# Attention on one Trainium2 core: value products for four heads at once, and softmax sums from one product of added probabilities

## The chip, the cores and the metric

The kernel runs on one core of a Trainium2 chip. The metric is the time on the device in microseconds (us), start to end of the program. The engines are TensorE (PE), VectorE (DVE), ScalarE (ACT), GpSimd (POOL) and SyncE (SP), which here only issues transfers. An instruction stream is one per engine, in order; the engines meet through semaphores.

## What is computed

A two-layer model on 4 batches of 512 tokens, width 512. The part that matters here is the attention of the second layer: 16 query heads in 4 groups, which share 4 key and value heads of 32 columns, with a linear bias by distance and a key mask. Cut from the reference:

```python
# _L1_xattn_ref: Q per query head, K and V per group, one group per key head
...
scores = scores + m * rel[None, None, None]
neg = jnp.finfo(scores.dtype).min
scores = jnp.where(mask[:, None, None, None, :], scores, neg)
w = jax.nn.softmax(scores, axis=-1)
out = jnp.einsum('bghqk,bkgd->bqghd', w, V)
out = out.reshape(b, q_len, G * Hpg * dh)
return out @ Wo
...
x = x + jnp.tanh(g_xattn[1]) * _L1_xattn_ref(_layernorm(x, axis=-1), ctx_2048, ctx_2048, mask_BxS2_bf1, L1_xattn_Wq, L1_xattn_Wk, L1_xattn_Wv, L1_xattn_Wo)
```

Before it come a cross attention stand-in (a product of quantised matrices) and a ternary feed-forward; after it a mixture of experts. The change touches neither.

## The kernel before

**Blocks and steps.** `stage_attention` works through 16 blocks: 4 batches times 4 values of j; a block is the four heads g = 0..3 that have their own key head g and query head j. A block has 8 steps (`BLOCK = 2 * KB`), a batch 32 (`STEPS`). In the kernel before, a step treats one pair of heads (`PAIRS = ((0, 2), (1, 3))`) and one key tile k of 128 keys: steps 0 to 3 are the four key tiles of the first pair, steps 4 to 7 those of the second.

**A step on PE** (L1355 to L1378) makes the two score matmuls of its pair, keys down and queries across, into `p_col` (L1371); between and after them it makes some of the *row scores* of a later block (`row_scores`, L1321), queries down, only to find each query's maximum; then the value products of the step before (`values`, L1334), and at last the fills of this step. There are two buffers each of `p_col` and `p_row`, so PE waits for ACT's exponential of the step before, and for DVE's maximum of two row scores before. How many row scores a step makes is in `ROWS_AT`; those from step 5 on (`AHEAD`) are for the block after the next.

**Value products.** `v1` holds for each key tile and head 32 columns of values and 32 columns of ones, in f32. Each head's product has 64 output partitions, 32 of the output and 32 of the sum of the probabilities, so two heads fill the 128 partitions of `p_out[pr]`, accumulated over four key tiles:

```python
for c, g in enumerate(PAIRS[pr]):
    mm = nc.tensor.matmul(p_out[pr][c * 2 * DH:(c + 1) * 2 * DH, :], v1[b % 2][:, k, g, :], prob[n % 4][:, c, :],
                          start=(k == 0), stop=(k == KB - 1))
```

**ACT** makes an exponential of 128 x 512 for each score matmul (L1240) into one of four `prob` buffers, copies `p_out` out (`take_out`, L1226), and the high f16 halves of fills. **DVE** makes the maxima of the row scores (`maxima`, L1438), the low halves of fills (`low`), the statistics and normalisation of the next batch's x (L1388 to L1400), and the inverse of the sums (`inverse`, L1451). **POOL** multiplies the output by the inverse and splits it into two f16 halves (`normalise`, L1160 to L1169). **SP** takes the sums out to memory, brings them back spread over 128 partitions, takes the inverses out, and spreads them over the head's rows (`sums_out`, `sums_spread`, `inverse_out`, `inverse_rows`); it also places the maxima (`place_top`, L1080) and the halves of queries and keys (`place`, L1073) into the operands of the scores.

**Fills** (`attention_fills`, L929) are work of the next batch (transposes of the context and x, the products for keys k, values v and queries q) and of the batch before (the output product, y), given to steps of the batch by the tables `NEXT` and `RESULT`. "top" is the transposition of a block's maxima, at step 4. y of a batch waits until POOL has normalised its last block.

**End.** The last block's inverse is made by DVE directly from the copied sums (`last_inverse`, two of its four halves in the last steps) and `last_normalise` multiplies the heads one by one (L1464).

## Time and profile before

| | us |
|---|---|
| median of 3 runs (1326.04 to 1329.34) | 1326.54 |
| the profiled execution, its own time | 1324.98 |
| its span, first to last instruction | 1323.3 |
| PE busy in the span | 1088.6 (82%) |
| DVE busy | 751.8 (57%) |
| ACT busy | 664.9 (50%) |
| POOL busy | 460.1 (35%) |
| granted clock of PE, mean | 0.931 |

The profile is of one execution; 1.7 us of its time lie around its span. The attention blocks stand from 369.9 to 728.0 us of the span. A busy time counts each moment in which the engine has an instruction in work; matmuls overlap, so a mean length of one can be larger than what it adds. The granted clock is 1.00 for 2.4 GHz and 0.5 for 1.2 GHz, averaged over the stretch. A wait is put down to the instruction whose signal came last.

### The profile page before, as it was taken

Reading aid. Unit: us, or ns where it says so; the run is one execution under the profiler, and the core shown is the slowest. Engines: PE = TensorE matmul, PEld = TensorE weight load, DVE = VectorE, ACT = ScalarE, POOL = GpSimd, SP = SyncE. Lnnn points to the kernel's source line nnn. Section 1 sums busy time; section 2 is a strip of 40 time slices with the busy share of each in tenths; the row PEclk is TensorE's granted clock in tenths of the full one; section 3 lists DMA queues with packets and bytes.
Section 4 is the critical chain, followed back from the end, with each engine's and each line's share of the span. In section 5 each row is a group of like instructions: output and inputs, shape, how many; then the busy total and the mean of one; then the engine's idle time right before and its main releaser. Section 6 shows DMA issues by size and latency. Waiting matters only on the chain. (4 is left out here: it accounts for less than half of the span.)

```text
span 1323.3 us, 19258 instructions
## 1 busy us (share of the span) xinstructions
PE 1088.6 (82%) x6093; PEld 520.5 (39%) x6111; DVE 751.8 (57%) x1420; ACT 664.9 (50%) x1010; POOL 460.1 (35%) x503
## 2 busy tenths in 40 slices
PE   0567788896699999999999467899997999999910
PEld 0343444453233343243232133444444566566600
DVE  6889867756786674665653466443333435443224
ACT  6888878794156665655667154212212344334400
POOL 1102443323102332322333303435006888882054
PEclk9978899998989999999999778799998999999965
DMA  9126600001102111110110122024003454442256
GB/s 336 45 96 196 257 0 1 1 1 40 37 23 68 37 40 54 40 37 22 41 31 18 45 74 66 1 96 181 1 0 114 150 162 166 150 156 93 71 170 227
DMA packets 66573, 110.62 MB, mean 84 GB/s; under 512 B 16756, under 2 KB 28660, under 8 KB 65992
## 3 DMA queue, kind: packets, MB, share of 16 engines
q1 hardware_dynamic: 56952, 77.63, 18.2%
q0 software_dynamic: 9264, 31.92, 7.6%
q8 instruction: 37, 0.61, 0.2%
q14 instruction: 32, 0.26, 0.1%
q10 hardware_dynamic: 288, 0.20, 0.1%
HBM read 68.44 MB, written 33.28 MB: 77 GB/s over the span
## 5 line engine op out<-in xcount | busy, mean ns | idle before, releaser
L1240 ACT ACTIVATE prob<-p_col,mask_col,any_key 128x512 f32<-128x512 f32 x256 | 185.7, 778 | 110.4 <-PE p_col L1371 108.9
L1438 DVE CUSTOM_DVE_ANT_0 ajunk<-p_row,mask_row 128x512 bf16<-128x512 f32 x256 | 166.8, 685 | 70.8 <-PE p_row L1321 70.8
L1334 PE MATMUL p_out<-prob,v 128*64 128x512 f32 x512 | 139.0, 621 | 0.1
L1321 PE MATMUL p_row<-ks,early_place 99*128 99x512 f16 x256 | 99.3, 389 | 13.4 <-DVE top L1438 11.9
L1160 POOL TENSOR_TENSOR o<-sum_a,rec 32x512 f32<-32x512 f32 x30 | 37.9, 1264 | 195.2 <-DMA rec<-inv_d 193.0
L1371 PE MATMUL p_col<-early_place,ks 101*128 101x512 f16 x256 | 95.5, 386 | 0.7 <-ACT prob L1240 0.3
L2290 DVE SCALAR_TENSOR_TENSOR shid<-s_up,ssilu 128x352 f32<-128x352 f32 x39 | 20.5, 525 | 122.1 <-PE s_up L2236 122.1
L2258 PE MATMUL s_down<-mw,shT 128*128 (+1 forms) x351 | 82.2, 379 | 1.1 <-ACT shT L2198 1.1
L2236 PE MATMUL s_gate<-mw,sxT 128*128 x468 | 78.3, 318 | 4.2 <-ACT sxT L2204 3.3
L2236 PE MATMUL s_up<-mw,sxT 128*128 x468 | 76.7, 314 | 0.0
L1851 PE MATMUL p_gate<-mw 128*128 128x512 f16 (+1 forms) x288 | 71.7, 402 | 1.2 <-ACT mw L1737 1.2
L1867 PE MATMUL p_down<-mw 128*128 128x512 f16 (+1 forms) x288 | 64.9, 384 | 9.4 <-DVE x L1956 9.4
L2292 DVE TENSOR_TENSOR shidr<-shid,shidr 128x352 f16<-128x352 f32 x39 | 59.7, 1532 | 21.5 <-ACT shidr L2188 21.5
L2151 POOL TENSOR_TENSOR mw<-mstg,mw 128x1408 f32 (+5 forms) x28 | 63.2, 2258 | 8.4 <-POOL mstg L2147 8.4
L1851 PE MATMUL p_up<-mw 128*128 128x512 f16 (+1 forms) x288 | 66.1, 379 | 0.0
L2180 ACT ACTIVATE ssilu<-s_gate 128x352 f32<-128x352 f32 x39 | 18.1, 463 | 95.2 <-PE s_gate L2236 95.2
L525 PE MATMUL po<-ctxT,xT 128*128 128x512 f32 x128 | 63.5, 646 | 0.0
L570 PE MATMUL po<-w2T,ctxT 128*128 128x512 bf16 x241 | 57.1, 379 | 7.7 <-DVE ctxT L791 4.9
L553 PE MATMUL pair<-w1T,q1T 128*128 128x512 bf16 x254 | 59.8, 379 | 1.4 <-DVE w2T L731 1.2
L2236 PEld LDWEIGHTS s_gate<-mw,sxT 128*128 128x128 f16 x468 | 43.8, 99 | 42.1 <-issue 21.8
L1758 ACT ACTIVATE silu<-p_gate,ebias 128x512 f32<-128x512 f32 (+1 forms) x24 | 16.3, 683 | 86.2 <-PE p_gate L1851 86.2
L2146 POOL TENSOR_TENSOR mw<-mstg,up 128x1408 f32 (+5 forms) x28 | 56.3, 2011 | 5.9 <-DMA mstg<-in_L_ffn_gate_w 5.4
(305 smaller groups left out, 2151.6 us busy)
## 6 DMA issues: line engine op xcount, KB each, us to landing
x_slots<-nought SPq DMA_DIRECT2D x3, 3328.0 KB, 19.8
...
```

What stands on the lines that cost most here:

```text
L525: mm = nc.tensor.matmul(po[t % 2][:], xT[b % 2][:, k, t * P:(t + 1) * P], ctxT[b % 2][:, k, :], start=(k == 0), stop=(k == KB - 1))
L553: mm = nc.tensor.matmul(ph[n][:, c:c + D], q1T[:, k, :], w1T[:, k, n * HALF + c:n * HALF + c + D], start=(k == 0), stop=(k == KB - 1))
L1240: nc.scalar.activation(prob[s % 4][:, c, :], p_col[c][:], ACT.Exp, bias=mask_col[:, b, k:k + 1], scale=any_key[:, b:b + 1]).then_inc(t_exp, 1)
L1321: nc.tensor.matmul(p_row[g % 2][:], qs[0:ROWS_R, j, g, t * P:(t + 1) * P], ks[b % 2][0:ROWS_R, g, :], start=True, stop=True).then_inc(t_ro ...
L1334: mm = nc.tensor.matmul(p_out[pr][c * 2 * DH:(c + 1) * 2 * DH, :], v1[b % 2][:, k, g, :], prob[n % 4][:, c, :], start=(k == 0), stop=(k == ...
L1371: nc.tensor.matmul(p_col[c][:], ks[b % 2][0:ROWS_C, g, k * P:(k + 1) * P], qs[0:ROWS_C, j, g, :], start=True, stop=True).then_inc(t_col, 1)
L1438: nc.vector.tensor_tensor_reduce(junk[:, g % 2, :], p_row[g % 2][:], mask_row[:, blk // HPG, :], 1.0, -3e38, ALU.add, ALU.max, top[blk % 2 ...
L1851: mm = nc.tensor.matmul(bank[i % 2][0:rows(m), :], unit(SHARED + n, hs, at + k * EI + m * P, rows(m)), xT[:, hm, k, g * S:(g + 1) * S], st ...
L1867: mm = nc.tensor.matmul(p_down[t % 2][:], hT[n][hs][0:rows(m), m, t * P:(t + 1) * P], unit(SHARED + n, hm, D0 + m * D, D, rows(m)), start= ...
L2151: nc.gpsimd.tensor_tensor(half(e, 1, q), s, half(e, 0, q), ALU.subtract).then_inc(m_wl, 1)
L2236: mm = nc.tensor.matmul(bank[n][:], xT[n][:, hs, k, :], w[:, bass.ds(e * (2 * WC) + c, EI)], start=(k == 0 and hs + hm == 0), stop=(k == K ...
L2258: mm = nc.tensor.matmul(p_down[n][:], hT[n][0:rows(m), hs, m, :], w[0:rows(m), bass.ds(e * (2 * WC) + c, D)], start=(m == 0 and hs + hm == ...
```

## The change

**Steps by key tile.** `PAIRS` is now ((0, 1), (2, 3)), and steps 2k and 2k + 1 treat the two pairs on key tile k. The value products of a key tile are made for all four heads together, once in two steps, in four matmuls of 32 output partitions each, without ones columns, into one `p_out`. There are six `prob` buffers.

**Sums.** The probabilities of the four key tiles are added before they meet PE: POOL adds tiles 0 and 1 (`add_first`, two instructions of 128 x 1024), DVE adds tiles 2 and 3 (`add_next`, four of them). PE multiplies the result by ones in four matmuls into `p_den`, at step 3 of the next block (`SUMS_AT`), ACT copies it (`take_sums`), and one transfer takes the sums out. In the last block tile 3 goes to PE without having been added.

**Also moved:** the tables of fills and rows, POOL's normalisation is one instruction instead of four, DVE's inverse is at step 7 instead of 5, some placings of queries go ahead of the inverses on SP, and the end is made from the new buffers. `v` is plain, 128 columns.

```diff
-    NEXT = {0: ("ctx", 0), 1: ("ctx", 1), 2: ("ctx", 2), 3: ("ctx", 3), 6: ("k", 0), 8: ("x", 0), 9: ("x", 1), 10: ("x", 2),
-            9.5: ("v", 0), 10.5: ("x", 3), 11: ("q", 0), 22: ("q", 1), 26: ("q", 2)}
-    RESULT = {13: 0, 15: 1, 17: 2, 19: 3}
-    OWN_Q, TOP_AT = 4, 4
+    NEXT = {0: ("ctx", 0), 1: ("ctx", 1), 2: ("ctx", 2), 3: ("ctx", 3), 7: ("k", 0), 8: ("x", 0), 9: ("x", 1), 9.5: ("x", 2),
+            10: ("x", 3), 12: ("q", 0), 23: ("q", 1), 25: ("q", 2), 29: ("v", 0)}
+    RESULT = {15: 0, 17: 1, 19: 2, 21: 3}
+    OWN_Q, TOP_AT = 5, 4
...
-    ROWS_AT = (2, 2, 2, 2, 0, 3, 3, 2)
+    ROWS_AT = (1, 3, 2, 2, 0, 3, 2, 3)
     AHEAD = 5
+    SUMS_AT = 3
...
+    def pair_of(blk, k, pr):
+        return prob[(BLOCK * blk + 2 * k + pr) % PROBS]
+    def heads(pr):
+        return prob_sum[:, 2 * pr:2 * pr + 2, :]
...
             def sums_out(n):
-                sp.wait_ge(t_outa, n + 1)
-                sp.dma_start(den_d[n % 2, 0:GROUPS:2, :], sum_a[n % 2][DH:P:2 * DH, :]).then_inc(t_den, 16)
                 sp.wait_ge(t_outb, n + 1)
-                sp.dma_start(den_d[n % 2, 1:GROUPS:2, :], sum_b[n % 2][0:P:2 * DH, :]).then_inc(t_den, 16)
+                sp.dma_start(den_d[n % 2], den_row[0:P:DH, :]).then_inc(t_den, 16)
...
+                for f in soon:
+                    place(f)
                 if blk:
                     inverse_out(blk - 1)
                     inverse_rows(blk - 1)
...
             def normalise(n):
                 pool.wait_ge(t_rec, 64 * (n + 1))
+                pool.wait_ge(t_outa, n + 1)
...
-                for g in range(GROUPS):
-                    q = slice(g * DH, (g + 1) * DH)
-                    nc.gpsimd.tensor_tensor(o[q, :], (sum_a, sum_b)[g % 2][n % 2][q, :], rec[q, :], ALU.mult).then_inc(t_scaled, 1)
...
+                nc.gpsimd.tensor_tensor(o[:], taken[n % 2][:], rec[:], ALU.mult).then_inc(t_scaled, 1)
...
+            def add_first(blk):
+                need(pool, t_over, blk)
+                for pr in range(2):
+                    pool.wait_ge(t_exp, 2 * (BLOCK * blk + 2 + pr + 1))
+                    pool.nop(nofuse=True)
+                    nc.gpsimd.tensor_tensor(heads(pr), pair_of(blk, 0, pr)[:], pair_of(blk, 1, pr)[:], ALU.add).then_inc(t_addp, 1)
             for blk in range(BLOCKS + 1):
+                if blk < BLOCKS:
+                    add_first(blk)
                 if blk > 1:
                     normalise(blk - 2)
...
+            def take_sums(n):
+                act.wait_ge(t_over, n + 1)
+                need(act, t_den, 16 * n)
+                nc.scalar.copy(den_row[:], p_den[:]).then_inc(t_outb, 1)
+            def prob_free(i):
+                blk, inb = divmod(i - PROBS, BLOCK)
+                k, pr = divmod(inb, 2)
+                act.wait_ge(t_pv, KB * blk + k + 1)
+                if k < 2:
+                    act.wait_ge(t_addp, 2 * blk + pr + 1)
+                else:
+                    act.wait_ge(t_addd, 2 * ((KB - 2) * blk + k - 2) + pr + 1)
...
                     if inb == 1 and blk:
-                        take_out(blk - 1, 1)
-                    if inb == KB + 1:
-                        take_out(blk, 0)
+                        take_out(blk - 1)
+                    if inb == SUMS_AT + 1 and blk:
+                        take_sums(blk - 1)
...
             def values(n):
...
+                pe.wait_ge(t_exp, 4 * (n + 1))
...
+                for g in range(GROUPS):
+                    q = slice(g * DH, (g + 1) * DH)
+                    mm = nc.tensor.matmul(p_out[q, :], v[b % 2][:, k, q], pair_of(blk, k, g // 2)[:, g % 2, :],
                                           start=(k == 0), stop=(k == KB - 1))
...
+            def sums(blk, of, start, stop):
+                for g in range(GROUPS):
+                    mm = nc.tensor.matmul(p_den[g * DH:(g + 1) * DH, :], ones[:, 0:DH], of(g), start=start, stop=stop)
+                return mm
+            def sums_of(blk):
+                pe.wait_ge(t_addd, 2 * (KB - 2) * (blk + 1))
+                need(pe, t_outb, blk)
+                sums(blk, lambda g: prob_sum[:, g, :], True, True).then_inc(t_over, 1)
...
-                    if s + b:
-                        values(STEPS * b + s - 1)
+                    if pr == 0 and s + b:
+                        values((STEPS * b + s) // 2 - 1)
+                    if inb == SUMS_AT and blk:
+                        sums_of(blk - 1)
...
+            def add_next(blk, k, pr):
+                i = 2 * ((KB - 2) * blk + k - 2) + pr
+                dve.wait_ge(t_exp, 2 * (BLOCK * blk + 2 * k + pr + 1))
+                if k == 2:
+                    dve.wait_ge(t_addp, 2 * blk + pr + 1)
+                else:
+                    dve.wait_ge(t_addd, i - 1)
+                dve.nop(nofuse=True)
+                nc.vector.tensor_tensor(heads(pr), heads(pr), pair_of(blk, k, pr)[:], ALU.add).then_inc(t_addd, 1)
...
-                    if inb == AHEAD and blk:
+                    if inb == BLOCK - 1 and blk:
                         inverse(blk - 1)
+                    if inb == 0 and blk:
+                        add_next(blk - 1, KB - 1, 1)
+                    if inb in (BLOCK - 3, BLOCK - 2):
+                        add_next(blk, KB - 2, inb - BLOCK + 3)
+                    if inb == BLOCK - 1 and blk + 1 < BLOCKS:
+                        add_next(blk, KB - 1, 0)
```

The order of the instructions, at three places. First PE, steps 5 and 6 of the second block. Before:

```order
L1371 MATMUL p_col<-early_place,ks 128x512
L1321 MATMUL p_row<-ks,early_place 128x512
L1371 MATMUL p_col<-early_place,ks 128x512
L1321 MATMUL p_row<-ks,early_place 128x512
L1334 MATMUL p_out<-prob,v_0 64x512 x2
L1321 MATMUL p_row<-ks,early_place 128x512
L1371 MATMUL p_col<-early_place,ks 128x512
L1321 MATMUL p_row<-ks,early_place 128x512
L1371 MATMUL p_col<-early_place,ks 128x512
L1321 MATMUL p_row<-ks,early_place 128x512
L1334 MATMUL p_out<-prob,v_0 64x512 x2
```

And now, the same two steps:

```order
L1430 MATMUL p_col<-early_place,ks 128x512
L1360 MATMUL p_row<-ks,early_place 128x512
L1430 MATMUL p_col<-early_place,ks 128x512
L1360 MATMUL p_row<-ks,early_place 128x512 x2
L1430 MATMUL p_col<-early_place,ks 128x512
L1360 MATMUL p_row<-ks,early_place 128x512
L1430 MATMUL p_col<-early_place,ks 128x512
L1360 MATMUL p_row<-ks,early_place 128x512
L1373 MATMUL p_out<-prob,v 32x512 x4
```

The value slot is gone from the odd step, and the even step's has four matmuls of 32 partitions for two of 64. (Before, one more row score followed the last row of its piece; step 7 makes it now.)

Second PE, steps 3 and 4 of the third block, where the sums of the block before are made (now):

```order
L1430 MATMUL p_col<-early_place,ks 128x512
L1360 MATMUL p_row<-ks,early_place 128x512
L1430 MATMUL p_col<-early_place,ks 128x512
L1360 MATMUL p_row<-ks,early_place 128x512
L1379 MATMUL p_den<-prob_sum,ones 32x512 x4
L1430 MATMUL p_col<-early_place,ks 128x512 x2
L1373 MATMUL p_out<-prob,v 32x512 x4
```

The slot of the sums stands in an odd step, where no value slot is.

Third DVE, steps 7 and 0 between the first two blocks (now; `ISA` is a maximum and the reading of its result, the addition is L1518):

```order
L1494 ISA ajunk,top<-p_row,mask_row 128x512
L1494 ISA top 128x1
L1494 ISA ajunk,top<-p_row,mask_row 128x512
L1494 ISA top 128x1
L1518 TENSOR_TENSOR prob_sum<-prob_sum,prob 128x1024
L1494 ISA ajunk,top<-p_row,mask_row 128x512
L1494 ISA top 128x1
L1518 TENSOR_TENSOR prob_sum<-prob_sum,prob 128x1024
L1479 SCALAR_TENSOR_TENSOR part_l<-p_fill,part_h 128x512
```

Before, nothing stood between the maxima there but the low halves of fills. On POOL a block's instructions were, and are now:

```order
L1160 TENSOR_TENSOR o<-sum_a,rec 32x512
L1160 TENSOR_TENSOR o<-sum_b,rec 32x512
L1160 TENSOR_TENSOR o<-sum_a,rec 32x512
L1160 TENSOR_TENSOR o<-sum_b,rec 32x512
L1167 TENSOR_SCALAR oT<-o 128x512
L1169 TENSOR_TENSOR oT<-o,oT 128x512
```

```order
L1189 TENSOR_TENSOR prob_sum<-prob 128x1024 x2
L1172 TENSOR_TENSOR o<-taken,rec 128x512
L1179 TENSOR_SCALAR oT<-o 128x512
L1181 TENSOR_TENSOR oT<-o,oT 128x512
```

Two additions of 1024 per partition have come before the normalisation, and four products of it have become one.

## Rows read from the trace of the kernel before

**Rows 1.** Windows, first batch: length, busy us of PE, PEld, DVE, ACT, POOL; PEclk, DMA.
```profile
369.90:395.60 25.70, 24.22 (x103) 8.38 (x103) 19.86 (x54) 15.40 (x25) 1.01 (x1) 0.90 0.08 22
395.60:419.80 24.20, 23.87 (x146) 9.95 (x145) 15.33 (x43) 15.35 (x25) 0.00 (x0) 1.00 0.25 77
419.80:438.90 19.10, 18.85 (x82) 5.43 (x81) 11.64 (x36) 13.48 (x20) 8.32 (x8) 1.00 0.16 38
438.90:458.50 19.60, 19.10 (x82) 5.52 (x81) 12.17 (x37) 13.54 (x21) 5.37 (x5) 1.00 0.13 36
```
**Rows 2.** The same view, second batch; the third repeats it within 0.5 us.
```profile
458.50:483.00 24.50, 23.45 (x110) 8.56 (x109) 18.79 (x55) 15.84 (x26) 10.21 (x9) 1.00 0.14 36
483.00:511.90 28.90, 28.65 (x170) 12.36 (x169) 16.37 (x45) 15.42 (x25) 7.01 (x7) 1.00 0.26 75
511.90:536.20 24.30, 24.05 (x106) 7.80 (x105) 12.82 (x39) 13.49 (x21) 5.74 (x6) 1.00 0.09 21
536.20:556.10 19.90, 19.05 (x82) 5.32 (x81) 12.15 (x37) 13.37 (x20) 5.41 (x5) 1.00 0.13 36
```
**Rows 3.** The same view, fourth batch, and the sum over all 16 blocks.
```profile
653.40:673.00 19.60, 19.26 (x82) 5.43 (x81) 12.95 (x36) 13.44 (x21) 6.84 (x6) 1.00 0.16 44
673.00:694.70 21.70, 21.45 (x94) 6.61 (x93) 12.54 (x37) 12.99 (x20) 10.23 (x9) 1.00 0.12 33
694.70:714.90 20.20, 19.84 (x85) 5.96 (x83) 7.59 (x22) 12.88 (x19) 3.43 (x4) 1.00 0.02 3
714.90:728.00 13.10, 12.69 (x49) 2.94 (x48) 3.11 (x3) 12.32 (x18) 7.34 (x7) 1.00 0.18 42
sum 358.10, PE 349.73 PEld 118.50 DVE 215.46 ACT 225.82 POOL 99.30; mean PE 21.86 PEld 7.41 DVE 13.47 ACT 14.11 POOL 6.21
```
**Rows 4.** Timeline of one step: start, length, instruction; and the value products as a group.
```profile
504.64 0.38 PE L1371 MATMUL p_col<-early_place,ks 101*128 101x512 f16 x1
...
504.68 1.45 ACT L1240 ACTIVATE prob<-p_col,mask_col,any_key 128x512 f32<-128x512 f32 x2 [2.39 <-PE p_col L1371]
504.86 0.38 PE L1321 MATMUL p_row<-ks,early_place 99*128 99x512 f16 x1
...
505.16 1.08 PE L1334 MATMUL p_out<-prob,v 128*64 128x512 f32 x4
...
506.18 0.39 PE L1321 MATMUL p_row<-ks,early_place 99*128 99x512 f16 x1
...
L1334 PE MATMUL p_out<-prob,v 128*64 128x512 f32 x512 | 139.0, 621 | 0.1
```
**Rows 5.** Timeline of the end of attention: DVE beside GpSimd (POOL).
```profile
733.37 2.52 DVE L1464 TENSOR_TENSOR xn<-sum_a,ramp 32x512 f32<-32x512 f32 x2
...
735.90 1.38 DVE L1464 TENSOR_TENSOR xn<-sum_b,ramp_i 32x512 f32<-32x512 f32 x2
```
**Rows 6.** Timelines in the experts' stage: one DVE addition alone, one beside GpSimd.
```profile
1155.36 0.53 DVE L2292 TENSOR_TENSOR shidr<-shid,shidr 128x352 f16<-128x352 f32 x1 [0.55 <-ACT shidr L2188]
...
1041.54 4.28 DVE L2292 TENSOR_TENSOR shidr<-shid,shidr 128x352 f16<-128x352 f32 x1 [0.55 <-ACT shidr L2188]
1041.55 2.54 POOL L2146 TENSOR_TENSOR mw<-mstg,up 128x1408 f32 x1
...
1044.05 1.38 POOL L2147 TENSOR_SCALAR mstg<-mstg 128x1408 f32<-128x1408 f32 x1
```
**Rows 7.** Groups of instructions on GpSimd in attention; one longer product (timeline).
```profile
L1160 POOL TENSOR_TENSOR o<-sum_a,rec 32x512 f32<-32x512 f32 x29 | 36.7, 1264 | 195.0 <-DMA rec<-inv_d 193.0
...
L1169 POOL TENSOR_TENSOR oT<-o,oT 128x512 f16<-128x512 f32 x14 | 16.2, 1157 | 1.2
...
1167.84 2.12 POOL L2151 TENSOR_TENSOR mw<-mstg,mw 128x1024 f32 x1 [0.31 <-POOL mstg L2147]
```
**Rows 8.** SP: four placings of the maxima (timeline); a transfer's time to landing.
```profile
500.96 2.47 SPq L1080 DMA_DIRECT2D early_place<-top_rows  x4
...
rec<-inv_d SPq DMA_DIRECT2D x60, 64.0 KB, 2.0
```

108 lines of the change are left out of this document (52 added, 56 removed).

## The prediction

> **What bounds the kernel now.** I read the windows first, one per block of attention [rows 1, 2, 3]. In every block the busy time of TensorE (PE) is 0.2 to 1.5 us short of the block's length, at a granted clock of 1.00 after the first: PE is the bound, while the vector engine (DVE) works 7.6 to 19.9 us of a block (3.1 of the last), the scalar engine (ACT) 12.3 to 15.9 and GpSimd at most 10.3. Over the 16 blocks the sum row has 349.7 us of PE in 358.1: 8.4 us idle, all there is to win without taking work from PE. The blocks differ: the second of a batch holds the most fills and takes 28.9 us, the fourth a single query fill and 19.9 [rows 2]; DVE is fullest in the first of a batch (18.8 of 24.5 us), where the statistics, the normalisation and the low halves of the context fall. Then the price of a value product, from one step on PE [rows 4]. Score matmuls start 0.22 us apart; from the one at 504.86 to the next at 506.18 are 1.32 us, so the value slot between costs 1.10. It holds four records (two matmuls, each in two passes) within 1.08 us, though the mean record is 0.62 us long: four in a row would not fit, so the two matmuls, on different columns, run side by side, and a slot costs what one would cost alone.
>
> **What the change takes from PE.** A block has 8 value slots now (4 key tiles, 2 pairs of heads) and will have 4, with four matmuls of 32 columns each, and one slot for the sums: 5 for 8. If four column groups run side by side as two do, a slot stays at 1.10, and a block of PE loses 3 x 1.10 = 3.3 us. Over the stage 128 slots (140.8 us) become 64 + 17 = 81 (89.1): 51.7 us less. The last block's saving is lost to ACT, see below. The price of a slot with four tiles is the first unknown. The rows bound it below by 1.10 (the same two passes), above by two turns: the slot less 0.14 for its edges, twice over, so 0.96 more: 2.06. I take 1.10, as the two matmuls start together and their ends make the slot.
> The Trainium skill ("TensorE: Matmul & The Clock Gate", Measured speedup vs the span model) gives 3.07x for four tiles by rows and 2.38x for three by columns; an estimate from that, 4 x 0.96 / 3.07, would make the slot 1.25 us and the stage's saving 40 us. No run here shows four tiles yet.
>
> **What it puts on DVE and GpSimd.** DVE adds four pairs (1024 values of two inputs in SBUF) per block. An addition of 352 took 0.53 us [rows 6], two of 512 took 1.38 [rows 5]: 0.16 us for 160 elements, so 0.69 + 0.51 = 1.20 for 1024, 4.8 per block. GpSimd adds two pairs; its products of 512 with f32 in and out take 1.26 us [rows 7]; a subtraction of 512 takes 1.16 and a product of 1024 takes 2.12 [rows 7], a factor of 1.83: 2.3 us each, 4.6 per block. Its normalisation falls from four products of 32 partitions to one of 128, 5.0 to 1.3 us, since it is paid by length. Its copy of 512 is some 0.6 by that of 1408 (1.38 [rows 6]). So GpSimd has 4.6 + 1.26 + 0.6 + 1.16 = 7.6 us per block; it is not a bound by itself.
> Now each block anew, by the larger of PE less 3.3 us and DVE plus 4.8, with the fills that the tables move (keys and queries stay in their block; v, 48 matmuls of 0.056 = 2.7 us, goes from the second block to the fourth; one product y, 12 matmuls = 2.6 us, from the second to the third). A batch in the middle [rows 2]: first block PE 20.2, DVE 23.6; second 20.1 and 19.6; third 23.4 and 18.4; fourth 18.5 and 17.7. That is 23.6 + 20.1 + 23.4 + 18.5 = 85.6 for 97.6 before, twice: 171. The first batch [rows 1]: 23.5 + 19.3 + 16.4 + 18.5 = 77.7 for 88.6 (DVE leads in three). The last [rows 3]: 17.8 + 16.6 + 19.2, and 12.5 for the block without rows, where ACT is busy 12.3 of 13.1: 66.1 for 74.6. Sum 315 for 358.1: **43 us less**. By PE alone (DVE left out) it would be 51.
>
> **What it gives back.** Three waits are new.
> First, DVE and GpSimd. Where both read SBUF with two operands, the trace shows them shutting each other out. An addition of DVE that takes 0.53 us alone took 4.28 when it began with GpSimd's product, to the end of that and of the next (2.54 + 1.38) [rows 6]. In the tail two products of DVE took 2.52 beside GpSimd and the next two, alone, 1.38 [rows 5]. The maxima of DVE read PSUM and are not held up. This is the rule that speaks against this change; the Trainium skill has it ("SBUF — State Buffer", SBUF: two separate sides): a lock for the whole instruction, against DVE instructions with two SBUF inputs; the trace agrees (4.28 us). GpSimd is busy 7.6 of some 19.7 us, and an addition that finds it so waits half an instruction, about 0.9 us weighted by length: 0.39 x 0.9 x 4 = 1.4 us per block, of which I let 1.0 fall on the path, 15 blocks: +15.
> Second, the exponentials. A value slot used to stand in every step; now steps with 1.0 us of PE alternate with steps of 2.1, against 1.45 us of ACT for two exponentials [rows 4], and there are only two score buffers. In the last block, where no rows are left, a step takes 13.1 / 8 = 1.64 us [rows 3] though PE needs 0.44 + 1.10 and ACT 1.45: 0.1 to 0.2 us of handing over. For some 45 steps without a fill, at 0.15: +7.
> Third, SP. The sums go out after step 4 instead of step 1, and the four placings of the next block's maxima stand behind them on SP, as before, but they used to go out before the maxima are transposed at step 4, and now go out after. From the copy: a transfer out and one back in, issue 0.6 each and 2.0 to land, of which the placings wait for the first; four placings 2.47, landing 2.0 [rows 8]: 0.6 + 2.0 + 0.6 + 2.47 + 2.0 = 7.7 us in the three steps left, 6.2 in a block of 16.5. Short by 1.5 in the three shortest blocks, none in the long ones: +4. The bounds are nothing, and 2 us in all 14 blocks (28).
> The end: four products of 0.69 with a lock-out, 3.9 us [rows 5], become one of 0.7; but the sums of the last key tile stand before the value product, and the normalisation of the block before ends later: -2 (0 to -4).
> Costing nothing: the fill of ones on GpSimd (it is busy 1.0 of the first block's 25.7 us [rows 1]), the second transfer of sums, the copy of v in one piece.
> **Sum:** -43 + 15 + 7 + 4 - 2 = -19 against the profiled execution's own 1324.98 us, 1306. The median of the runs is 1.6 higher than that execution: **1307 us**.
>
> **Rivals.**
> A, PE stays the bound: the additions fit in DVE's gaps, the waits fall away. -43 to -51 and the end: 1326.5 - 45 = 1281, or 1274 with 51. For it: DVE idles over 5 us in most blocks. Against it: PE has only two row buffers, so a DVE that is late by more than one step stops it.
> B, slower: **DVE's additions are shut out by GpSimd's chain**. The order puts them in steps 5, 6, 7 and 0, and GpSimd's two additions and three normalising instructions run from step 3 or 4 on, nearly back to back. If each wait is that of [rows 6] (two instructions, 3.9 less the 0.5) or about 1.2 to 1.6 us on average, a block pays 4.8 to 6.4; all maxima stand behind the addition on DVE, all row products behind those on PE. It decides from 2.9 us per block on (43 / 15). With 4.8: 1326.5 - 43 + 72 + 7 - 2 = 1360. Against it: the new instructions of GpSimd each wait for a semaphore, and in such a gap DVE can enter.
> C, four tiles don't run side by side but two and two: 81 x 2.06 = 167 us for 140.8, +26, and the waits: 1353 to 1365.
> D, no change: placings, sums and the wait of the y products for the normalisation (now due in the same step 15) eat the 19 us: 1322 to 1330. GpSimd frees the probability buffers too; the six hold three key tiles, which gives it about 3 us of room.
> E, a slot a little longer than 1.10, by 0.15: 81 x 0.15 = 12 us less taken from PE, of which half counts, in the blocks that PE leads: 1313, inside the forecast's range. The skill's figure above would give about this.
>
> **How the numbers follow.** Forecast 0.52 (E in it), A 0.22, B 0.12, C 0.05, D 0.09. A measurement of this kernel can tell 0.3%, 4 us. Faster by more: forecast, A, and a little of D, 0.75. Same 0.08. Slower: B, C, and some of D, 0.17. The likeliest case's own range is 1292 to 1320 (waits of 10 to 38 us instead of 26). The range: down to 1277, which leaves out the lowest of A; up to 1328, which leaves out B and C: 1277 to 1328.
>
> **What would show it.** The p_out records should come eight to a slot of 1.1 us; a slot near 2.1 is C. DVE should be over 90% busy in the first block of each batch, and the additions should have a median of 1.2 us with a tail to 2 or 3 where GpSimd runs; a median over 2.4 is B. PE should wait for DVE's maxima far more than now, and for ACT in steps without a fill. SP's placings should follow the sums at once, without waiting for ACT. If the stage from the first exponential to the last is shorter than 320 us, the waits were overrated; over 350, DVE or the feeds bind. A PE clock under 1.00 in the stage would make all of it wrong.

## The result and the profile after

The changed kernel takes **1378.8 us** (median of 4 runs, 1378.5 to 1381.8) for 1327.1 before (4 runs): a ratio of 1.039, 95% interval 1.037 to 1.041. It is slower by 52 us, where the prediction had it faster by 19, and lies far outside the range. The profiled execution took 1381.8 us, its span is 1380.1. From the page of the changed kernel, the engines' busy time (before, DVE had 751.8 and PE 1088.6):

```profile
PE 1076.7 (78%) x6229; PEld 516.6 (37%) x6247; DVE 860.8 (62%) x1473; ACT 665.9 (48%) x1010; POOL 482.1 (35%) x488
```

The windows by block, the view of [rows 1 to 3]: the second batch (compare [rows 2]), the last two blocks of the kernel, and attention as a whole, from the start of its first exponential to the end of its last (358.1 us before [rows 3]):

```profile
478.70:511.50 32.80, 23.63 (x118) 8.54 (x117) 28.45 (x62) 15.46 (x24) 8.65 (x6) 0.90 0.06 15
511.50:538.80 27.30, 22.76 (x118) 8.15 (x116) 23.02 (x46) 15.95 (x25) 7.67 (x5) 0.94 0.27 81
538.80:565.20 26.40, 23.65 (x126) 8.18 (x124) 20.83 (x43) 12.95 (x20) 7.68 (x5) 1.00 0.09 24
565.20:591.10 25.90, 19.91 (x137) 8.58 (x136) 19.67 (x39) 13.87 (x22) 7.66 (x5) 0.93 0.14 39
...
750.60:771.40 20.80, 19.32 (x105) 6.33 (x103) 15.58 (x28) 12.92 (x19) 9.41 (x5) 1.00 0.07 15
771.40:784.80 13.40, 9.93 (x55) 2.09 (x54) 6.40 (x3) 12.23 (x18) 7.77 (x4) 1.00 0.09 22
...
375.70:784.80 409.10, 328.26 (x1743) 112.92 (x1741) 328.41 (x668) 225.75 (x341) 123.81 (x75) 0.93 0.12 32
```

Attention takes 409.1 us for 358.1: 51.0 more, and that is the whole loss. PE is busy 21.5 us less, but idle 80.8 us instead of 8.4. DVE's busy time rose by 113 us, far more than 62 additions of 1.2 us (74). PE's granted clock, at 1.00 in all but the first block before, is 0.93 on average: PE not only stands more, it is also slower in part of the time in which it works. Behind attention both profiles take 595.3 us. (Attention began 5.8 us later in this execution than in the profiled one before. The medians differ by 51.7 us, about as much as attention alone, so these 5.8 us are not put down to the change.)

Where DVE's time went, by tile: minimum, median and maximum in ns of the two instructions that split the maxima (`split_tops`) and of DVE's and GpSimd's additions. Before, the first two had 203 and 229 as their medians.

```profile
L1501 DVE CAST topb<-top x16: 203/1631/2212, 367.1 to 760.4; 128x16 f16<-128x16 f32 x16
L1502 DVE TENSOR_TENSOR topb<-top,topb x16: 229/2292/2351, 367.4 to 760.6; 128x16 f16<-128x16 f32 x16
...
L1518 DVE TENSOR_TENSOR prob_sum<-prob_sum,prob x62: 1159/1220/3302, 393.2 to 783.6; 128x1024 f32<-128x1024 f32 x62
...
L1189 POOL TENSOR_TENSOR prob_sum<-prob x32: 2337/2356/2373, 383.3 to 780.3; 128x1024 f32<-128x1024 f32 x32
```

The additions cost what the forecast said (1.22 us, 2.36 on GpSimd, a tail to 3.3 where they meet). The split, two instructions over 16 values each, takes 3.9 us instead of 0.43, nine times as long. The timeline of the first block of the second batch shows why:

```profile
489.63 4.66 POOL L1189 TENSOR_TENSOR prob_sum<-prob 128x1024 f32<-128x1024 f32 x2 [18.30 <-PE p_den L1379]
...
490.38 1.06 PE L1373 MATMUL p_out<-prob,v 128*32 128x512 f32 x8
...
490.57 1.48 DVE L1501 CAST topb<-top 128x16 f16<-128x16 f32 x1
...
492.08 2.29 DVE L1502 TENSOR_TENSOR topb<-top,topb 128x16 f16<-128x16 f32 x1
494.25 1.27 POOL L1172 TENSOR_TENSOR o<-taken,rec 128x512 f32<-128x512 f32 x1
...
494.52 0.38 PE L1317 MATMUL p_fill<-identh,topb 128*128 128x128 f16 x4 [3.08 <-DVE topb L1502]
```

The product of the sums, in step 3, releases GpSimd's two additions of the next block; they start 0.9 us before DVE comes to the split of step 3. The split's first instruction ends with GpSimd's first addition, its second with the second. PE stands at the transposition of the maxima for 3.1 us, and ACT behind PE. What follows is slower too: PE's granted clock is 1.00 up to this wait, 0.76 from 494.5 to 498.0 us and 0.71 in the 3 us after. The value slot at 490.38 holds eight records (four matmuls, each in two passes) in 1.06 us: four tiles run side by side, for what two cost before [rows 4]. The waits in attention, three of them (us in total, times, longest; before, ACT waited 108.9 us here, the row products 7.4 and the fill of the maxima not at all):

```profile
ACT prob L1278 <- PE p_col L1430: 141.6, 76, 6.5
...
PE p_row L1360 <- DVE top L1494: 48.4, 46, 2.5
...
PE p_fill L1317 <- DVE topb L1502: 23.7, 11, 3.6
```

### The profile page after: what moved, and what is told of

It reads as the page before. It is cut to its first block and busy times, and to the rows that moved or that the text cites. A ratio compares the mean times of both kernels' runs of the same rounds, so it can differ in the third digit from the quotient of the medians.

```text
span 1380.1 us, 19615 instructions
## 1 busy us (share of the span) xinstructions
PE 1076.7 (78%) x6229; PEld 516.6 (37%) x6247; DVE 860.8 (62%) x1473; ACT 665.9 (48%) x1010; POOL 482.1 (35%) x488
## 5 line engine op out<-in xcount | busy, mean ns | idle before, releaser
L1189 POOL TENSOR_TENSOR prob_sum<-prob 128x1024 f32<-128x1024 f32 x32 | 74.7, 2355 | 301.0 <-PE p_den L1379 175.9
L1360 PE MATMUL p_row<-ks,early_place 99*128 99x512 f16 x256 | 107.3, 423 | 57.9 <-DVE top L1494 51.6
L1430 PE MATMUL p_col<-early_place,ks 101*128 101x512 f16 x256 | 98.6, 397 | 3.6 <-ACT prob L1278 2.6
L1518 DVE TENSOR_TENSOR prob_sum<-prob_sum,prob 128x1024 f32<-128x1024 f32 x62 | 82.5, 1332 | 8.1 <-POOL prob_sum L1189 7.0
L1373 PE MATMUL p_out<-prob,v 128*32 128x512 f32 x512 | 72.3, 639 | 0.2 <-ACT taken L1248 0.2
L2356 DVE TENSOR_TENSOR shidr<-shid,shidr 128x352 f16<-128x352 f32 x39 | 58.1, 1490 | 21.5 <-ACT shidr L2252 21.5
L1360 PEld LDWEIGHTS p_row<-ks,early_place 99*128 99x128 f16 x256 | 25.7, 101 | 117.8 <-DVE top L1494 101.5
```

The costliest lines, as they stand in the source:

```text
L1189: nc.gpsimd.tensor_tensor(heads(pr), pair_of(blk, 0, pr)[:], pair_of(blk, 1, pr)[:], ALU.add).then_inc(t_addp, 1)
L1360: nc.tensor.matmul(p_row[g % 2][:], qs[0:ROWS_R, j, g, t * P:(t + 1) * P], ks[b % 2][0:ROWS_R, g, :], start=True, stop=True).then_inc(t_ro ...
L1373: mm = nc.tensor.matmul(p_out[q, :], v[b % 2][:, k, q], pair_of(blk, k, g // 2)[:, g % 2, :], start=(k == 0), stop=(k == KB - 1))
L1430: nc.tensor.matmul(p_col[c][:], ks[b % 2][0:ROWS_C, g, k * P:(k + 1) * P], qs[0:ROWS_C, j, g, :], start=True, stop=True).then_inc(t_col, 1)
L1518: nc.vector.tensor_tensor(heads(pr), heads(pr), pair_of(blk, k, pr)[:], ALU.add).then_inc(t_addd, 1)
L2356: ins = nc.vector.tensor_tensor(hidr[:, 1, :], hid[:], hidr[:, 0, :], ALU.subtract)
```

## The experiments

Theory L: GpSimd's additions shut DVE out of its split of the maxima. Theory W: DVE has too much work, its additions stand in front of the maxima. Later theories stand where they came up. The kernels ran on several chips, and on some of them the kernels, the one before included, are some 22 us slower, behind attention as far as the profiles show (last section). So this table compares attention in the profiled executions, in us, and the kernel's time only with the kernel before in the same comparison. The expectations of x3, x1, x2 and e5 give kernel times as on the first chip; there the kernel before took 24 us less than beside these four runs.

| kernel | attention | PE busy | DVE busy | PE clock | kernel | before, there |
|---|---|---|---|---|---|---|
| before | 358.0 | 349.7 | 215.4 | 0.99 | | |
| before, again (b0) | 359.1 | 350.8 | 215.3 | 0.99 | 1329.7 | 1329.2 |
| **after** | **409.1** | 328.3 | 328.4 | 0.93 | 1378.8 | 1327.1 |
| x3: no additions | 353.9 | 308.6 | 214.4 | 0.97 | 1348.2 | 1351.0 |
| x1: DVE's alone | 375.3 | 320.4 | 284.6 | 0.94 | 1362.8 | 1351.0 |
| x2: GpSimd's alone | 384.6 | 322.1 | 256.3 | 0.94 | 1378.7 | 1351.0 |
| e5: GpSimd's after the split | 395.8 | 327.2 | 294.0 | 0.92 | 1384.4 | 1351.0 |
| p1: x3, sums sent early | 353.5 | 311.8 | 214.5 | 0.96 | 1326.0 | 1329.2 |
| s1: p1, halved slots | 353.5 | 321.8 | 214.2 | 0.96 | 1324.1 | 1329.2 |
| x4: x3, one value product | 350.7 | 297.0 | 213.8 | 0.91 | 1348.3 | 1354.0 |
| x5: x3, half exponentials | 350.7 | 307.1 | 213.1 | 0.98 | 1344.7 | 1354.0 |
| x6: x3, half maxima | 341.2 | 307.7 | 155.3 | 0.97 | 1332.0 | 1354.0 |
| x7: x4 and x6 | 340.7 | 290.9 | 155.5 | 0.91 | 1308.0 | 1329.0 |
| x8: x5 and x6 | 335.3 | 306.9 | 155.6 | 0.97 | 1324.2 | 1348.8 |
| f1: x3, split fills | 355.9 | 309.4 | 214.2 | 0.97 | 1352.8 | 1354.0 |
| r1: x3, fills first | 359.0 | 317.8 | 213.8 | 0.95 | 1334.2 | 1329.0 |
| h2: DVE two additions | 380.7 | 344.8 | 250.5 | 0.96 | 1347.6 | 1329.2 |
| g2: GpSimd two additions | 368.3 | 339.5 | 213.0 | 0.97 | 1336.7 | 1329.0 |
| g4: g2, fills first | 365.4 | 339.0 | 212.8 | 0.97 | 1334.2 | 1329.0 |
| g5: g4, GpSimd's order turned | 389.8 | 348.1 | 217.2 | 0.95 | 1377.0 | 1348.8 |

**b0**, the kernel before once more.

> The kernel before, unchanged, once more with a profile. On the chip of the first four experiments it took 1351 us, 24 more than on the chip of the first comparison. In the experiments that time lies behind attention (from its last exponential to the end: 612 to 619 us there, 595.3 both before and after the change on the first chip). If that is the chip's doing, attention takes 358 us here as on the first chip, within 1.5 us, and lengths of attention can be compared over all runs.

Attention takes 359.1 us on another chip, 358.0 on the first; its first block has 1.1 of the difference. Both are chips of the quicker kind: no kernel was profiled on both kinds. For the slower ones the evidence is indirect. x3 (slower) and p1 (quicker), which differ in one number, have 353.9 and 353.5 us. And in every run here the difference in attention to before and the difference of the whole kernel to the kernel beside it agree within 6 us, so a difference of a few us between chips is not safe.

### Whose additions cost what: x3, x1, x2

x3 leaves out every addition, x1 GpSimd's, x2 DVE's:

```diff
 # x3 and x1: GpSimd
-                if blk < BLOCKS:
-                    add_first(blk)
 # x3 and x2: DVE
-                    if inb == 0 and blk:
-                        add_next(blk - 1, KB - 1, 1)
...
```

> Left out: all additions of probabilities, GpSimd's and DVE's; the sum product of TensorE is still made, from ones written once, so the sums are wrong values of the right shape. Everything else of the change stays: four-tile value slots, one sum slot per block, the later placings. Theory L (the loss is GpSimd's additions shutting out DVE's split of the maxima at step 3, with the top fill on TensorE behind it) and theory W (DVE simply has too much work, and the additions stand as bursts in front of the maxima) both expect what the value slots alone are worth: stage 307 to 320 us, kernel 1275 to 1290 us, split_tops back to 0.20 and 0.23 us. A third theory, P (the placings and the sums that go out after step 4, or the hand-over between TensorE and ACT, cost by themselves), expects the stage to stay above 340 us and the kernel above 1310.

> Left out: the first key tile's share of the sums, and with it both additions on GpSimd; DVE still makes its four additions a block (its first takes key tiles 1 and 2 from the probabilities). Theory L expects that the split at step 3 falls from 1.63 + 2.29 us to about 0.2 + 0.23, the waits of the row product and of the top fill go back, and the kernel takes 1310 to 1325 us (the 40 us that the lock-out is put at, and some more of DVE's other waits). Theory W expects that most of the loss stays, since DVE has the same additions at the same steps: 1350 us or more, with DVE's maxima still waited for by some 80 us.

> Left out: key tiles 2 and 3 in the sums, and with them the four additions on DVE; the small reciprocal of the sums on DVE is an addition of 1 instead. GpSimd still adds key tiles 0 and 1 in steps 3 and 4. Theory L expects the split still stretched to over 1.2 us for each of its two instructions and the top fill still waiting for it, so most of the loss stays, less what the four additions cost: 1325 to 1350 us. Theory W expects the loss gone with DVE's 4.8 us a block: 1280 to 1300 us.

Attention as one window, in x3, x1 and x2, in this order (length, busy us of PE, PEld, DVE, ACT, POOL, then PEclk):

```profile
375.60:729.50 353.90, 308.56 (x1751) 106.36 (x1749) 214.36 (x607) 224.21 (x341) 45.70 (x45) 0.97 0.14 37
```
```profile
373.30:748.60 375.30, 320.41 (x1751) 108.94 (x1749) 284.62 (x669) 225.38 (x341) 47.43 (x45) 0.94 0.13 35
```
```profile
373.20:757.80 384.60, 322.05 (x1751) 111.16 (x1749) 256.30 (x607) 225.32 (x342) 118.46 (x76) 0.94 0.13 34
```

The four corners of one square: with no additions 353.9, DVE's add 21.4, GpSimd's 30.7, both 55.2. Their costs add up but for 3.1 us, so L and W are both right, each for its part, and neither is all of it. With the 24 us taken off, x1 took 1339 us, between L's 1325 and W's 1350, and x2 1355, 5 over L's range and far from W's 1300: each theory misses its numbers. And x3 misses the number of both, and has that of P (over 340). Without one addition attention is 354 us, 4 less than before, though PE has 41 us less to do; it should have been 307 to 320.

The split in x2, the tile view:

```profile
L1499 DVE CAST topb<-top x16: 202/1640/2236, 364.6 to 733.4; 128x16 f16<-128x16 f32 x16
L1500 DVE TENSOR_TENSOR topb<-top,topb x16: 229/2291/2349, 364.9 to 733.7; 128x16 f16<-128x16 f32 x16
```

Stretched without DVE's additions as with them; in x1 and x3 the medians are 0.20 and 0.23. The lock-out is GpSimd's alone, and shows in DVE's busy time: 256.3 for 214.4 us, 41.9 more with the same number of instructions. PE's top fill waits 24.9 us for it in x2, 0.5 in x1.

### Keeping GpSimd off the split: e5

```diff
                 need(pool, t_over, blk)
+                if blk + 1 < BLOCKS:
+                    pool.wait_ge(t_top, blk + 2)
```

> The whole computation; one wait is added: GpSimd starts its two additions of a block only after DVE has split the next block's maxima (step 3). Theory L expects the split back at 0.2 and 0.23 us in nearly all blocks, the top fill no longer waiting for it (23.7 us of wait now), and 1330 to 1345 us: some 40 us less than the changed kernel, of which the later additions of GpSimd, now beside those of DVE, may take some back. Theory W expects no gain or a small one: 1365 to 1380 us.

Ratio to before 1.026 (1.022 to 1.030), for 1.039: a third of the loss is gone, and 13.3 us of attention, where L had 40. With the 24 us taken off it is 1360 us, between L's 1345 and W's 1365. The split is back (tile view), and two other waits have come:

```profile
L1503 DVE CAST topb<-top x16: 202/204/208, 361.9 to 741.3; 128x16 f16<-128x16 f32 x16
L1504 DVE TENSOR_TENSOR topb<-top,topb x16: 228/230/234, 362.2 to 741.6; 128x16 f16<-128x16 f32 x16
```
```profile
PE p_row L1362 <- DVE top L1496: 61.6, 52, 3.4
...
DVE xn L1464 <- POOL arstd L1152: 9.3, 3, 4.2
```

That GpSimd shuts DVE out of the split is shown by this and by x1 and x2. Why so little comes back is read from the trace: GpSimd now starts and ends later, and so do DVE's own additions, which need GpSimd's and stand in front of the maxima. PE waits 61.6 us for maxima, 48.4 in the changed kernel. In a batch's first block GpSimd's one power over four values (`arstd`), which stands behind its additions, makes DVE wait as well. Moving the split to GpSimd was not tried.

### Why the thinner PE gains nothing: p1, s1, x4, x5, x6, x7, x8, f1, r1

All leave out the additions, and are compared with x3, 353.9 us.

p1 sends the sums two steps earlier (`SUMS_AT = 1` for 3); s1 also spreads the work evenly over the steps:

```diff
-    ROWS_AT = (1, 3, 2, 2, 0, 3, 2, 3)
+    ROWS_AT = (2, 2, 2, 2, 0, 3, 3, 2)
...
+                    if inb == 2:
+                        values((STEPS * b + s) // 2 - 1)
+                    if inb >= KB:
+                        values((STEPS * b + s) // 2 - 1, pr)
```

> Left out as in the run without additions: all additions of probabilities, so the sums are wrong values. Beside that run one number changes: the sum product stands in step 1 instead of 3, so the sums go out on SP before the next block's maxima are transposed, as in the kernel before. Theory P (the placings stand behind the sums' two transfers on SP and come late for the next block): the waits of the column product for the transferred top rows (7.5 us on TensorE, 9.0 on its loads, in 4 places) go, attention shortens by 8 to 12 us from 353.9. Theory S (steps are bound one by one, by two exponentials of 0.78 or three maxima of 0.77 us, so the TensorE time saved in the steps without a value slot is lost there) expects 0 to 5 us.

> Left out: all additions, so the sums are wrong values. Beside the run before it here (sum product in step 1), the value products of key tiles 1 and 2 are cut into two halves of 256 queries, one in the step with the slot and one in the step after, and the row products of a block stand two to a step again as before the change (2, 2, 2, 2, 0, 3, 3, 2): the same work, spread evenly over steps. Theory S expects the last four steps of a block without a fill at 1.6 to 1.8 us each instead of 2.0 to 2.3 in the even ones, and attention 10 to 20 us shorter than the run before it. If TensorE's sum of work or the waits for SP bound the blocks, as the prediction's sum by blocks has it, it gains nothing (within 4 us).

Both take 353.5 us, where P had 8 to 12 us less than x3 for p1, and S 10 to 20 less than p1 for s1. Both fall as they were put, but neither test is clean. In p1 PE still waits 5.1 us for the placing of the maxima (7.5 in x3) and 3.8 for one of the queries, as in x3: DVE's inverse stayed at step 7. In s1 the halved products raise PE's busy time by 10 us (321.8 for 311.8), which may hide a gain from the even steps.

Then one engine's work at a time was cut down:

```diff
 # x4: only key tile 0 in full
-                    mm = nc.tensor.matmul(p_out[q, :], ... pair_of(blk, k, g // 2)[:, g % 2, :],
+                    mm = nc.tensor.matmul(p_out[q, 0:w], ... pair_of(blk, k, g // 2)[:, g % 2, 0:w],
 # x5: half of each exponential
-                        nc.scalar.activation(pair_of(blk, k, pr)[:, c, :], p_col[c][:], ACT.Exp, ...
+                        nc.scalar.activation(pair_of(blk, k, pr)[:, c, 0:S // 2], p_col[c][:, 0:S // 2], ACT.Exp, ...
 # x6: half of each maximum
-                nc.vector.tensor_tensor_reduce(junk[:, g % 2, :], p_row[g % 2][:], ...
+                nc.vector.tensor_tensor_reduce(junk[:, g % 2, 0:S // 2], p_row[g % 2][:, 0:S // 2], ...
```

> Left out: all additions of probabilities and, of the value products, those of key tiles 1, 2 and 3, but for 2 of 512 queries each, so attention's result is wrong. Against the run without additions (attention 353.9 us) TensorE has 3 x 0.8 to 1.1 us less to do in each of 16 blocks. If TensorE's work still bounds the blocks, attention falls by 35 to 50 us, to 305 to 320. If the steps are bound by the exponentials on ACT, the maxima on DVE and the hand-over through two buffers each, with the fills of 2.6 us as lumps between them in which both starve, it falls by less than 15 us.

> Left out: all additions, and the exponentials of half of the queries (256 of 512 in each of the 256 instructions; the rest of the probabilities is 1), so attention's result is wrong. ACT loses 256 x 0.25 to 0.33 us of 224. If ACT is what binds a thinned step, attention shortens by 15 to 40 us from 353.9; if TensorE or DVE does, by less than 8.

> Left out: all additions, and half of each row's maximum (256 of 512 keys, not below 0), so that the exponents are shifted wrongly. DVE loses 240 x 0.25 to 0.3 us of 214. If DVE's maxima bind a thinned step, attention shortens by 15 to 40 us from 353.9; if TensorE or ACT does, by less than 8.

They gain 3.2, 3.2 and 12.7 us: x4 and x5 as if TensorE and ACT did not bind, x6 between its two readings (under 8, over 15). The first block of the last batch, which has no loads of a next batch in it, shows the steady state; before, it took 19.60 us with PE busy 19.26 [rows 3]. The windows of x3, x4, x6 and x8 there, one after the other:

```profile
653.50:671.80 18.30, 16.45 (x89) 4.67 (x90) 11.74 (x37) 13.36 (x21) 3.04 (x3) 1.00 0.11 32
```
```profile
650.40:667.70 17.30, 14.69 (x89) 4.59 (x90) 11.94 (x39) 13.18 (x20) 3.04 (x3) 1.00 0.15 38
```
```profile
636.70:653.90 17.20, 16.19 (x89) 4.88 (x90) 8.09 (x39) 13.40 (x20) 3.04 (x3) 1.00 0.14 36
```
```profile
639.60:656.50 16.90, 16.26 (x90) 4.67 (x90) 8.30 (x37) 10.13 (x21) 3.04 (x3) 1.00 0.12 34
```

Five slots for eight gave PE 2.8 us and the block 1.3 (19.6 to 18.3): even here PE has gaps of 1.9 us now. Three value products more (x4) give 1.0 for 1.8 of PE, and halving the maxima (x6) 1.1: nobody is the bound alone. And where ctx and statistics are loaded, in the first block of the third batch, x3 and x6:

```profile
558.70:583.50 24.80, 20.59 (x118) 7.79 (x116) 20.28 (x57) 15.45 (x25) 4.05 (x4) 1.00 0.10 24
```
```profile
547.20:569.40 22.20, 20.41 (x118) 7.79 (x117) 15.59 (x57) 15.44 (x25) 4.02 (x4) 1.00 0.12 30
```

24.8 us with PE at 20.6, for 24.5 with PE at 23.45 before: three us less of PE, and nothing gained. (In the first and second batch this block is 0.8 and 0.6 us shorter than before.) With half the maxima it is 22.2, so 2.6 us of it are DVE's, which is busy 20.3 us of x3's 24.8.

x4 also shows what the clock takes back. The last block of all, in x3 and in x4:

```profile
716.20:729.50 13.30, 10.92 (x63) 2.23 (x62) 0.25 (x1) 12.19 (x18) 3.05 (x3) 1.00 0.08 22
```
```profile
711.70:726.70 15.00, 12.03 (x63) 2.40 (x62) 0.26 (x1) 12.13 (x18) 3.05 (x3) 0.68 0.06 20
```

With less work PE is busy longer, 12.0 us for 10.9, at 0.68 instead of 1.00: the granted clock fell to its lower level of 1.2 GHz for a part of the block. Over attention x4's clock is 0.91 for 0.97, which is part of why its PE is busy only 11.5 us less. So x4 bounds the gain of still thinner value products on this chip; it doesn't show what they would give at a full clock.

x7 joins x4 and x6, x8 joins x5 and x6.

> Left out: all additions, the value products of key tiles 1 to 3 but for 2 queries, and half of each maximum; the two single cuts gave 3.2 and 12.8 us of 353.9. If TensorE and DVE bound in turn, step by step (each cut alone only uncovers the other), both together give clearly more than 16 us: attention 310 to 330. If the gaps come from something else (ACT, transfers, the clock), they give 16 us or less: 338 or more.

> Left out: all additions, half of the exponentials and half of each maximum; TensorE has the work of the run without additions (attention 353.9 us). Each cut alone gave 3.2 and 12.8 us. The forecast's sum has TensorE alone at 307 to 318 us here. If ACT and DVE bound the thinned steps in turn, the two cuts together give more than their sum: attention 312 to 332 us. If it takes 336 us or more, neither is what keeps TensorE waiting, and the gaps come from the transfers, the order of the queues and the clock.

x7 is 13.2 us shorter than x3, of which x6 alone had 12.7; by its expectation the gaps then come from something else, though its clock of 0.91 blurs this as in x4. x8 is 18.6 shorter, 2.7 more than x5 and x6 together, and falls between its two bounds (332 and 336). So half of the exponentials and half of the maxima stand for about half of the 36 us between the forecast's 318 and x3's 353.9, and hardly in turn. What PE still waits for in x8:

```profile
PE p_row L1358 <- DVE top L1492: 13.7, 42, 1.0
PE p_col L1428 <- DMA early_place<-top_rows: 8.8, 4, 4.8
PE p_row L1358 <- DMA early_place<-part_l: 4.3, 1, 4.3
```

The rest, then, is not free of DVE (13.7 us), and 13.1 us are waits for SP's placings, of which PE had none before. One of these waits can be followed to something that the forecast left out of its sum: DVE's inverse stands at step 7 and no longer at 5. In the second block of the last batch SP sends the inverses out at 672.5 us in x3, before at 668.7. The placings of the queries behind them end at 684.1 for 680.2, and a row product waits 3.8 us for them. No run puts the inverse alone back to step 5; in h2 (below), where more is changed, it is there, and PE waits for no placing at all. How much of the 36 us the placings make stays open. Two other guesses failed. The fills of 2.6 us were issued in two halves (f1), or ahead of the row products beyond the first two (r1):

```diff
 # f1
-                        fill_(f)
+                        if f.kind in "kqvy":
+                            fill_(f, 0)
+                            halves.append(f)
+                        else:
+                            fill_(f)
 # r1
-                    next_rows(4)
                     for f in fills_at(b, s):
                         fill_(f)
+                    next_rows(4)
```

> Left out: all additions. Against the run without additions (353.9 us) one thing is changed: the fills of 12 matmuls or more on TensorE (keys, queries, values, results: 2.6 us each, in one lump at a step's end, 42 of them in attention) are issued in two halves, the second in the next step behind its first column and row product. If the lumps cost by starving ACT and DVE (their two buffers cover about 1.5 us), attention shortens by 0.5 to 1 us a lump, 20 to 40 us. If TensorE's sum of work or another engine's binds, by less than 8 us.

> Left out: all additions. Against the run without additions (attention 353.9 us) two lines change places on TensorE: in each step the fills are issued before the row products beyond the first two, and no longer behind them. Theory R (the third row product of a step waits for a row buffer, that is for one of DVE's maxima of 0.77 us, and what stands behind it in TensorE's queue waits too: the fill, and behind the fill the column products that ACT needs) expects the waits of TensorE's row products for DVE (29.4 us, 42 times) to fall by more than half and attention to take 325 to 343 us. If those waits are covered anyway, it takes 349 us or more.

f1 is 2 us longer than x3, r1 5. The waits in r1, where x3 has 7.5 and 29.4 us in the same two rows:

```profile
PE p_col L1425 <- DMA early_place<-top_rows: 16.4, 4, 7.3
...
PE p_row L1355 <- DVE top L1489: 11.1, 31, 0.8
```

The wait that r1 was made to remove fell by 18 us, and attention grew; PE waits 9 us more for the placing of the maxima, and is busy 9 us longer at a clock of 0.95 for 0.97. As I read it, later row products mean a later split and a later placing; no run tests that by itself. Theory R falls.

### Can the saving be had? h2, g2, g4, g5

Four versions with the whole computation. In all of them PE makes three sum products a block (key tiles 0 + 1 added, 2, 3) in steps without a value product, 7 slots for 8 before, and two row products to most steps. g4 is g2 with r1's exchange. In h2 ACT also copies the sums at step 2, and DVE's inverse is at step 5 again; the others leave it at 7. Who adds the first two tiles differs:

```diff
 # h2, DVE in step 4
+                    if inb == KB:
+                        add_first(blk, 0)
+                        add_first(blk, 1)
 # g2, GpSimd after the split
+                if blk + 1 < BLOCKS:
+                    pool.wait_ge(t_top, blk + 2)
...
+                    if inb in (1, SUMS_AT) and blk:
+                        sums_of(blk - 1, KB - 2 + k)
+                    if inb == BLOCK - 1:
+                        sums_of(blk, 1)
```

> The whole computation, another division of the sums: GpSimd adds nothing; DVE adds key tiles 0 and 1 (two additions of 1.2 us a block, both in step 4, in which it has no maxima); TensorE makes three sum products a block, from that sum, key tile 2 and key tile 3, in the steps 5, 7 and 1 that have no value product. So each step but step 3 has one slot, 7 a block for 8 before the change; row products two to a step as before. By theories L and S: TensorE saves 1.1 us a block, nothing is locked out, no step is overfull: attention 340 to 352 us, 6 to 18 us less than before the change, and the kernel faster than before by 0.3 to 1.3%. By theory W (additions in front of DVE's maxima are what costs, 5.1 us per addition and batch as in the run without GpSimd's additions, where four cost 21 us) the two cost 10 us and the gain is 0 to 8 us.

> The whole computation: DVE adds nothing; GpSimd adds key tiles 0 and 1 as in the change, but only once DVE has split the next block's maxima; TensorE makes three sum products a block (that sum in step 7, key tiles 2 and 3 in steps 1 and 3 of the next block), so 7 slots a block for 8 before the change; row products two to a step as before. Theory L expects no stretched split (0.20 and 0.23 us) and little else of DVE stretched, since its maxima are not held up: attention 343 to 358 us (no additions 353.9, with 2 slots more). If GpSimd's additions hold up something else of DVE, or the two slots come on top, 362 to 380 us.

> The whole computation: the run before it with the fills ahead of the surplus row products on TensorE. Theory R expects it 3 to 12 us shorter than that run; with less rows in three-row steps than in the run without additions the gain is smaller here. Below 350 us of attention the kernel is faster than the one before the change. If theory R is wrong, the two differ by less than 3 us.

h2: 1.014 (1.010 to 1.018), attention 380.7 us, where L and S had 340 to 352 and W at most the 358 of before. The additions, 2.4 us in a row and more where GpSimd runs beside them, keep the maxima of step 5 back, and the sum product, which waits for them 13.5 us in all, keeps back the fill. g2: 1.006 (1.004 to 1.008), g4: 1.004 (1.003 to 1.006): against the kernel before in the same comparison, which makes them some 45 us better than the change and 5 to 8 short of the kernel before. g2's attention of 368.3 us misses L's 343 to 358, though the split is back at 0.20 and 0.23 us: it is in the range of the other reading, that GpSimd holds up something else or the two slots come on top, and the run does not tell these apart. g4's attention is 2.9 us shorter, on the border between what R and its denial had; one execution each does not settle that. In g4 PE waits 7.4 us for placings, before not at all, and the inverse is at step 7 there too; putting it back was not tried. What else is left in g4 shows in the first block of the third batch:

```profile
574.86 4.68 POOL L1192 TENSOR_TENSOR prob_sum<-prob 128x1024 f32<-128x1024 f32 x2 [12.47 <-DVE topb L1507]
...
576.34 0.91 DVE L1462 TENSOR_SCALAR aveps<-amv 128x4 f32<-128x4 f32 x1
...
579.48 1.28 POOL L1172 TENSOR_TENSOR o<-taken,rec 128x512 f32<-128x512 f32 x1
...
582.79 1.02 POOL L1152 TENSOR_TENSOR arstd<-aveps,neg_half 128x4 f32<-128x4 f32 x1
583.85 1.00 DVE L1467 TENSOR_SCALAR xn<-x,amv,arstd 128x512 f32<-128x512 f32 x2 [3.71 <-POOL arstd L1152]
...
585.51 0.61 PE L1363 MATMUL p_row<-ks,early_place 99*128 99x512 f16 x1 [3.93 <-DVE top L1499]
```

A power over four values per partition, whose input is there at 577.3, stands behind two additions and a normalisation; DVE waits for it, PE for DVE, and the block takes 28.8 us for 24.5 before. The DVE instruction that makes the power's input (`aveps`) is held as well: its median is 0.90 us in g4 for 0.17 before, and the one shown runs beside the additions.

g5 turns GpSimd's order:

```diff
-                if blk < BLOCKS:
-                    add_first(blk)
                 if blk > 1:
                     normalise(blk - 2)
+                if blk < BLOCKS:
+                    add_first(blk)
```

> The whole computation: the last version (attention 365.4 us) with two lines of GpSimd's order turned: the normalisation of the block before last stands ahead of a block's two additions and no longer behind them, so that the power (arstd), for which DVE's normalisation of the next batch waited 3.7 us at most in each batch's first block, is ready some 3 us earlier, and the probabilities' buffers come free without a wait of ACT (3.0 us). If that queueing on GpSimd is what makes a batch's first block 28.8 us instead of 24.5, attention takes 350 to 358 us and the kernel is 0.1 to 0.6% faster than before the change. If the additions themselves are in the way there, it stays within 4 us of 365.

A miss: 1.019 (1.016 to 1.021). The block in question came down (25.0 and 27.5 us), but each batch's third block went up, in the third batch from 26.1 to 32.9 us. There the normalisation waits for the result products that still read its `oT` buffer, the additions now stand behind it, and ACT behind the additions:

```profile
645.70 0.62 POOL L1179 TENSOR_SCALAR oT<-o 128x512 f16<-128x512 f32 x1 [8.74 <-DVE x L1492]
...
647.51 4.64 POOL L1192 TENSOR_TENSOR prob_sum<-prob 128x1024 f32<-128x1024 f32 x2
649.94 1.45 ACT L1281 ACTIVATE prob<-p_col,mask_col,any_key 128x512 f32<-128x512 f32 x2 [7.25 <-POOL prob_sum L1192]
```

The power alone ahead of the normalisation, with the additions left in front, was the smaller edit and was not tried. No version here with the whole computation beats the kernel before.

## Why the prediction was wrong, step by step

**The prices** were right. A value slot is 1.06 us of records for four tiles, so C and E fall. The value and sum products together take 52 us less in their rows (137.9 us before, 68.9 and 17.0 in x3), as forecast. An addition costs what was said (median 1.22 us, not over 2.4), so B falls as it was put, though the kernel is slower as B had it: the additions are not what is shut out.

**The sum by blocks** ("each block anew, by the larger of PE less 3.3 us and DVE plus 4.8") failed twice. Without additions it gives 307, with the exponentials' 7 and SP's 4 us 318; x3 measured 353.9, **36 us more**. PE's busy time fell by 41 us instead of 51, and its idle time rose from 8 to 45 instead of 19. Of the missing 10 us of PE, 6 are score and row products that take longer (94.3 and 88.3 us before, 96.8 and 91.7 in x3, at a clock of 0.97). A block at 97% on one engine says nothing of how short it gets when that engine is relieved: ACT and DVE were at 13 to 19 us of 20 to 24, behind two buffers each, and the first block of a batch with loads got shorter by 0.8 us at most. At least half of the 36 us is theirs (x8 cuts their work by half only); the clock and the waits for placings, which x3's trace shows too, are part of the rest, and how the rest divides is open.

And DVE's additions cost 21.4 us (x1) where the two sums, 51 and 43, leave 8 for them: **13 more**. Some 7 of the 13 are a slip in the sum. Its blocks set PE's busy time, less 3.3 us, against the old lengths, and so let the 8.4 us in which PE stood vanish; the 51 leaves 7 of them in (358.1 - 51 = 307, but 349.7 - 15 x 3.3 = 300). By its own rows DVE leads seven blocks, by 15 us in all. The other 6 us I read as the price of an addition of 1.2 us in front of maxima, which costs even where the block as a whole has room for it; x1 shows only the 21.4 in all.

**The lock** ("an addition that finds it so waits half an instruction", and +15 in all) had the mechanism and the wrong victim. I asked which of the new instructions meet GpSimd and forgot the old ones; the split, 0.43 us and in no row of mine, was never priced. GpSimd's additions cost 30.7 us alone (x2), 33.8 on top of DVE's, for the 15 forecast: **19 more**. The Trainium skill ("SBUF — State Buffer", SBUF: two separate sides) names beside instructions with two SBUF inputs those in a two-port performance mode; I had left out the second half. The trace agrees that it is not two inputs alone: a copy over 16 values, with one input, took 1.6 us, as its neighbour with two took 2.3; in which mode the copy ran no trace shows. Half the rule would have been enough here, as the split's second instruction has two inputs: applied to every DVE instruction in the steps that GpSimd's additions cover, it finds the place.

36 + 13 + 19 = 68: from the forecast's 341 for attention to the 409 measured.

**Smaller terms.** SP's placings: sending the sums early gave 0.4 us (p1), the forecast 4; but the later inverse, which the forecast did not price, is still in p1. The exponentials' 7 us were not tested by themselves; halving all exponentials gave 3.2 us (x5). The end: from the last exponential to the first result product 11.7 us, before 10.9; forecast 2 less, came 1 more. "A PE clock under 1.00 in the stage would make all of it wrong" was a sign set beforehand, and came true: 0.93. DVE was 87% busy in the first block of the second batch, where over 90 was expected, and PE waits for maxima far more, as told.
